# A one-core layer program whose separate preamble is spread over statistics, routing and experts

## What is computed

```python
x = x + 0.5 * ffn(layernorm(x), waff, W1, b1, W2, b2, threshold)
x = x + attn(layernorm(x), W_qkv, u_qkv, sigma_qkv, W_proj, u_proj, sigma_proj)
x = x + 0.5 * ffn(layernorm(x), waff, W1, b1, W2, b2, threshold)
```

```python
v = W @ u;    v = v / norm(v)
u2 = W.T @ v; u2 = u2 / norm(u2)
sigma = einsum('c,cd,d->', v, W, u2)
y = x @ (sigma_param[0] / sigma * W)
```

```python
num = einsum('bsd,ed->bse', inputs, waff)
aff = num / (norm(inputs) * norm(waff) + 1e-9)
cap = clip(floor(S * sigmoid(aff.mean() - threshold)), 4, S)
dispatch = one_hot(argmax(aff)) * (rank of aff in its sequence < cap)
for e in range(8):
    out += gelu((inputs * dispatch[e]) @ W1[e] + b1[e]) @ W2[e] + b2[e]
```

## Time and profile before

| what | us |
| --- | --- |
| median of 3 runs without profile | 1116.17 (1114.18 to 1118.52) |
| the profiled execution | 1130.24, of it the span 1128.4 |
| preamble, to the first load of x | 0.8 to 42.35 |
| statistics | 42.35 to 95.28 |
| routing | 95.28 to 165.87 |
| first experts, until PE's last dense stretch | 165.87 to about 330 |
| attention, settling of places, second experts | to the end |

### The profile page before, as it was taken

One profiled execution on the slowest core, in us unless ns is written; L12 is line 12 of the kernel. 1 busy time (PEld: TensorE's weight loads), 2 busy tenths in 40 slices (PEclk: granted clock), 3 DMA queues, 4 the chain that ended last, 5 costly groups with the idle time before them and its releaser, 6 DMA issues. The chain is left out here.

```text
span 1128.4 us, 26562 instructions
## 1 busy us (share of the span) xinstructions
PE 920.1 (82%) x8217; PEld 692.7 (61%) x8217; DVE 722.5 (64%) x2357; ACT 592.5 (53%) x1548; POOL 710.2 (63%) x1318
## 2 busy tenths in 40 slices
PE   2494636999965789999899998999999883799996
PEld 1383225999962456656556565565655552699995
DVE  6587953444423668887887878788888764344441
ACT  3023513666631456666666655666666561466663
POOL 4261975444303457888888877888888674155554
PEclk9755556999995989999999999999999995799998
DMA  5261002222314554554554545445455300222220
GB/s 168 84 189 32 1 5 45 68 68 68 64 41 94 99 90 91 95 115 93 100 113 92 101 88 103 95 97 115 94 104 108 70 22 23 69 65 67 59 66 22
DMA packets 127407, 89.72 MB, mean 80 GB/s; under 512 B 14305, under 2 KB 117910, under 8 KB 127270
## 3 DMA queue, kind: packets, MB, share of 16 engines
q1 hardware_dynamic: 104166, 53.24, 22.1%
q10 hardware_dynamic: 14400, 17.19, 7.9%
q0 software_dynamic: 8704, 17.60, 5.8%
HBM read 52.23 MB, written 35.47 MB: 78 GB/s over the span
## 5 line engine op out<-in xcount | busy, mean ns | idle before, releaser
L1529 DVE TENSOR_REDUCE at_mx<-at_pp 128x2 f32<-128x512 f32 (+1 forms) x384 | 261.8, 684 | 89.8 <-PE at_pp L1296 44.5
L1221 ACT ACTIVATE at_pt<-at_pm 128x512 f32<-128x512 f32 x384 | 228.7, 597 | 161.8 <-PE at_pm L1307 91.3
L1128 POOL TENSOR_SCALAR_AFFINE_SELECT at_pt<-at_pt 128x256 f32<-128x256 f32 (+1 forms) x384 | 184.8, 486 | 73.5 <-ACT at_pt L1221 69.9
L877 ACT ACTIVATE e_ht<-e_ps_h,b1t 128x128 f32<-128x128 f32 x576 | 164.2, 370 | 90.3 <-PE e_ps_h L905 78.1
L905 PE MATMUL e_ps_h<-e_xnt,e_w1own 128*128 128x128 f32 x1152 | 157.5, 281 | 7.0 <-issue 3.6
L915 PE MATMUL e_ps_y<-w,e_ht 128*128 x1152 | 160.3, 283 | 1.0 <-issue 1.0
L905 PEld LDWEIGHTS e_ps_h<-e_xnt,e_w1own 128*128 128x128 f32 x1152 | 144.9, 198 | 9.0 <-issue 7.3
L915 PEld LDWEIGHTS e_ps_y<-w,e_ht 128*128 128x128 f32 x1152 | 140.9, 193 | 2.2 <-issue 0.5
L961 DVE SCALAR_TENSOR_TENSOR e_y<-e_ps_y,e_x 128x256 f32<-128x256 f32 x72 | 30.6, 425 | 163.6 <-PE e_ps_y L915 163.6
L843 POOL DMA_INDIRECT out_dram<-e_y,e_x x72 | 73.9, 1026 | 94.7 <-DVE e_y L961 81.7
L827 POOL DMA_INDIRECT e_x<-rows,gidx x72 | 68.5, 951 | 75.0 <-DVE e_y L961 56.3
(11 more groups left out here) (331 smaller groups left out, 1802.1 us busy)
## 6 DMA issues: line engine op xcount, KB each, us to landing
at_qkd<-at_part SPq DMA_DIRECT2D x64, 192.0 KB
kb<-at_qkd SPq DMA_DIRECT2D x64, 96.0 KB
qs<-at_qkd ACTq DMA_DIRECT2D x64, 96.0 KB
e_x<-buckets SPq DMA_DIRECT2D x72, 66.0 KB
x<-e_y SPq DMA_DIRECT2D x36, 128.0 KB
rows<-ts_x ACTq DMA_DIRECT2D x16, 264.0 KB, 2.9
ts_x<-in_x_dram SPq DMA_DIRECT2D x16, 256.0 KB
x_by_token<-at_xa SPq DMA_DIRECT2D x32, 128.0 KB
```

The costliest lines, as they stand in the source:

```text
L877: last = a.activation(hid_t[j % NB][:, f, :], ps_h[j % NB][:, f, :], ACT.Gelu, bias=c.b1t[:, ds(e, 1), f])
L1128: g.affine_select(out=tile, in_=tile, compare_op=ALU.is_ge, fill=0.0, base=0, pattern=[[0, n], [1, P]], channel_multiplier=-1).then_inc(ma ...
L1221: a.activation(pt[u % RING][:, :], pm[u % 2], ACT.Exp, scale=SCALE).then_inc(exped, 1)
L1529: v.tensor_reduce(out, src, axis=AX.X, op=ALU.max).then_inc(maxed, 1)
```

## The change

The block `preamble` is gone. Its work stands elsewhere:

- In `token_stats` the ring has eight buffers. ACT's queue issues the ten small loads, the router weights and b1 first (semaphore `w_in`), the other eight counted by `s_in`. POOL makes the identity, the blank columns of the eight buffers and the iotas ahead of its roots, and the other constants after the root of one block or another (`constant`). DVE fills the small blanks before its first block, does `small` between the statistics of blocks 0 and 1, and a piece of the spectral norm after the normalization of most blocks (`spectral`). PE's small matmuls stand behind the projection of blocks 0, 4, 9 and 13. ACT takes gelu(b1) at the start and writes the constant rows of `kb` after blocks 4, 6, 8 and 10.
- In `route` SP loads w2 and w1 at the block's start. The 32 bias matmuls stand in groups of eight behind the inversions of groups 3 to 6, into PSUM that the counts no longer need; the sum over experts stands before the last inversion. DVE adds up behind its eight groups and makes the three parts after the expert numbers; SP then writes `cst`. Four small tiles now share memory with `den`, which is no longer needed there.
- In the first `experts` POOL blanks `kb`, `qs` and `vp`, 16 pieces, one behind the gathers of units 3 to 18 (`blank`). PE waits once for w2, DVE once for w1.
- The memsets of a ninth, empty expert in w1 and w2 are gone.

The diff, cut to this:

```diff
-        NX = 4
+        NX = 8
...
+            def power(n):
+                if n == 0:
+                    pool.wait_ge(early, 3)
+                    pool.wait_ge(powask, 1)
+                    g.tensor_tensor(c.wnorm[:, :], sq[:, :], half[:, :], ALU.pow).then_inc(pows, 1)
+                else:
+                    pool.wait_ge(powask, n + 1)
+                    g.tensor_tensor(col[:, 6 + 2 * n:8 + 2 * n], col[:, 4:6], mhalf[:, :], ALU.pow).then_inc(pows, 1)
+
+            def constant(b):
...
+                if b == 3:
+                    power(0)
+                if b == 7:
+                    power(1)
+                if b == 13:
+                    power(2)
...
                 g.tensor_tensor(c.xnorm[:, ds(b * TS, TS)], x_row[k][:, :, D + 1], x_row[k][:, :, D + 2], ALU.mult).then_inc(xnorm_done, 1)
+                constant(b)
...
+            a = nc.scalar
+            act.dma_start(waff_n[:, :], io["waff"]).then_inc(w_in, 16)
+            act.dma_start(b1_chunks[:, :], io["b1"].rearrange("e (c p) -> (e c) p", p=P)).then_inc(w_in, 16)
+            for dst, src in ((w_raw[:, parts[0]], io["wqkv"]), (w_raw[:, parts[1]], io["wproj"]),
+                             (u_row[:, parts[0]], io["uqkv"].partition_broadcast(P)), (u_row[:, parts[1]], io["uproj"].partition_broadcast(P)),
+                             (sig[:, 0:1], io["sqkv"].partition_broadcast(P)), (sig[:, 1:2], io["sproj"].partition_broadcast(P)),
+                             (c.thr[:, :], io["thr"].partition_broadcast(P)), (c.b2_rows[:, :], io["b2"])):
+                act.dma_start(dst, src).then_inc(s_in, 16)
+            act.wait_ge(filled, 4)
+            act.wait_ge(b1_t, 1)
...
+                if b in (4, 6, 8, 10):
+                    minus_one((b - 4) // 2)
...
+            def small():
...
+                dve.wait_ge(waff_tr, 1)
+                v.tensor_copy(c.waff_t[:, :], p_small[:, 0:E]).then_inc(waff_done, 1)
+                dve.wait_ge(waff_done, 1)
+                v.tensor_tensor(sq[:, :], c.waff_t[:, :], c.waff_t[:, :], ALU.mult).then_inc(ask, 1)
+
+            def spectral(b):
+
+                if b == 1:
+                    dve.wait_ge(picked, 2)
+                    v.tensor_reduce(sel_f[:, :], pick[:, :, :], axis=AX.X, op=ALU.add).then_inc(sel_done, 1)
+                    dve.wait_ge(told, 1)
+                    v.tensor_copy(sq[:, :], p_small[:, 16:16 + E]).then_inc(powask, 1)
+                    dve.wait_ge(s_in, 16 * 8)
+                    s.step(v.tensor_tensor(prod[:, :], w_raw[:, :], u_row[:, :], ALU.mult))
+                if b == 2:
+                    dve.wait_ge(sel_done, 1)
+                    for w in range(2):
+                        v.tensor_copy(sel[:, :, w], sel_f[:, :]).then_inc(selected, 1)
+                    s.step(sums(0))
+                if b == 3:
+                    v.tensor_tensor(col[:, 2:4], col[:, 0:2], col[:, 0:2], ALU.mult).then_inc(ask, 1)
+                if b == 5:
+                    dve.wait_ge(told, 2)
+                    v.tensor_copy(col[:, 4:6], p_col[:, 0:2]).then_inc(powask, 1)
+                if b == 8:
+                    dve.wait_ge(pows, 2)
+                    s.step(v.tensor_tensor(col[:, 0:2], col[:, 0:2], col[:, 8:10], ALU.mult))
+                    s.step(v.tensor_scalar(v_bc[0][:, :], c.ones[:, :], col[:, 0:1], None, ALU.mult))
+                    v.tensor_scalar(v_bc[1][:, :], c.ones[:, :], col[:, 1:2], None, ALU.mult).then_inc(ask, 1)
+                if b == 10:
+                    dve.wait_ge(told, 3)
+                    s.step(v.tensor_copy(u2[:, :], p_u2[:, :]))
+                    s.step(v.tensor_tensor(prod[:, :], u2[:, :], u2[:, :], ALU.mult))
+                if b == 11:
+                    sums(4).then_inc(powask, 1)
+                    dve.wait_ge(powask, 3)
+                    s.step(v.tensor_tensor(prod[:, :], w_raw[:, :], u2[:, :], ALU.mult))
+                if b == 12:
+                    s.step(sums(6))
+                    v.tensor_tensor(col[:, 2:4], col[:, 6:8], col[:, 0:2], ALU.mult).then_inc(ask, 1)
+                if b == 14:
+                    dve.wait_ge(told, 4)
+                    dve.wait_ge(pows, 3)
+                    s.step(v.tensor_tensor(col[:, 12:14], p_col[:, 0:2], col[:, 10:12], ALU.mult))
+                    s.step(v.reciprocal(col[:, 12:14], col[:, 12:14]))
+                    s.step(v.tensor_tensor(col[:, 14:16], col[:, 12:14], sig[:, :], ALU.mult))
+                if b == 15:
...
                 if not last:
                     stats(b + 1, (k + 1) % NX)
                 norm(b, k)
+                spectral(b)
...
+            def spectral(b):
+                if b == 0:
+                    pe.wait_ge(early, 1)
+                    pe.wait_ge(ask, 1)
+                    te.matmul(p_small[:, 16:16 + E], c.ones[:, :], sq[:, :], start=True, stop=True).then_inc(told, 1)
+                if b == 4:
+                    pe.wait_ge(ask, 2)
+                    te.matmul(p_col[:, 0:2], c.ones[:, :], col[:, 2:4], start=True, stop=True).then_inc(told, 1)
+                if b == 9:
+                    pe.wait_ge(ask, 3)
+                    for w in range(2):
+                        last = te.matmul(p_u2[:, parts[w]], v_bc[w][:, :], w_raw[:, parts[w]], start=True, stop=True)
+                    last.then_inc(told, 1)
+                if b == 13:
+                    pe.wait_ge(ask, 4)
+                    te.matmul(p_col[:, 0:2], c.ones[:, :], col[:, 2:4], start=True, stop=True).then_inc(told, 1)
...
                     project(b - 1, (k - 1) % NX)
+                spectral(b)
...
+            pe.wait_ge(eye, 2)
+            pe.wait_ge(w_in, 16 * 2)
+            te.transpose(p_small[:, 0:E], waff_n[:, :], c.ident[0:E, 0:E]).then_inc(waff_tr, 1)
+            te.transpose(p_b1[:, 0:E * FC], b1_chunks[:, :], c.ident[0:E * FC, 0:E * FC]).then_inc(b1_t, 1)
+            pe.wait_ge(waff_done, 1)
             run(step)
...
+        @blk.sync
+        def _(sp):
+            sp.dma_start(c.w2[:, 0:E, :, :], io["w2"].rearrange("e (c p) d -> p e c d", p=P)).then_inc(c.w2_in, 16)
+            sp.dma_start(c.w1[:, 0:E, :], io["w1"].rearrange("e d f -> d e f")).then_inc(c.w1_in, 16)
+            sp.wait_ge(const_split, 5)
+            for n in range(3):
+                sp.dma_start(c.cst[n:n + 1, :, :], c.const_parts[:, n, :].unsqueeze(1)).then_inc(c.cst_in, 16)
...
+            def bias_rows(q):
+
+                if q == 0:
+                    pe.wait_ge(c.w2_in, 16)
+                    pe.wait_ge(coords, 1)
+                for n in range(q * E, (q + 1) * E):
+                    last = te.matmul(own, c.gelu_b1[:, n * E:(n + 1) * E], c.w2[:, n // FC, n % FC, :],
+                                     start=(n == 0), stop=(n == E * FC - 1))
+                if q == FC - 1:
+                    last.then_inc(bias_sum, 1)
...
                 if g >= INV_LAG:
                     invert(g - INV_LAG)
+                if BIAS <= g < BIAS + FC:
+                    bias_rows(g - BIAS)
             for g in range(NG - INV_LAG, NG):
+                if g == NG - 1:
+                    pe.wait_ge(b2_done, 1)
+                    te.matmul(both, c.ones[0:E, 0:G], c.b2_rows[:, :], start=True, stop=True).then_inc(bias_done, 1)
...
             carry(NG - 1)
+            dve.wait_ge(zeroed, 1)
+            dve.wait_ge(bias_sum, 1)
+            v.tensor_copy(own_rows[0:E, :], own_of).then_inc(own_done, 1)
+            dve.wait_ge(own_done, 1)
+            v.tensor_tensor(c.b2_rows[:, :], c.b2_rows[:, :], own_rows[0:E, :], ALU.add).then_inc(b2_done, 1)
...
+
+            dve.wait_ge(bias_done, 1)
+            v.tensor_tensor(const_rows[:, :], both_of, own_rows[:, :], ALU.subtract).then_inc(const_done, 1)
+            dve.wait_ge(const_done, 1)
+            for n in range(3):
+                rows = const_rows if n == 0 else rest_rows
+                v.tensor_copy(c.const_parts[:, n, :], rows[:, :]).then_inc(const_split, 1)
+                if n < 2:
+                    dve.wait_ge(const_split, 2 * n + 1)
+                    v.tensor_tensor(rest_rows[:, :], rows[:, :], c.const_parts[:, n, :], ALU.subtract).then_inc(const_split, 1)
...
@@ -834,6 +859,8 @@
                     if j % 2 == 0:
                         pool.wait_ge(y_done, j // 2 + 1)
                     gather(j + 2 * NR)
+                    if j % 2 == 1 and 3 <= j // 2 < 3 + 4 * NQ:
+                        blank(j // 2 - 3)
...
             pe.wait_ge(c.cst_in, 16 * 3)
+            pe.wait_ge(c.w2_in, 16)
...
-        preamble(nc, m, io, c)
         token_stats(nc, m, io, c, io["x"])
-        route(nc, m, c, "r1")
+        route(nc, m, io, c, "r1")
```

352 lines of the change are left out of this document (126 added, 226 removed).

## The result

| | before | after |
| --- | --- | --- |
| median of the runs, us | 1117.35 (4 runs, 1114.18 to 1120.91) | 1081.67 (4 runs, 1080.78 to 1082.42) |
| the profiled execution | 1130.24 | 1081.78, of it the span 1080.0 |

The ratio is 0.9676, with a 95% interval of 0.964 to 0.9713: 35.7 us shorter, between 32 and 40. The forecast was 1084.4 in a range of 1076 to 1093, with 31.8 us less. So it holds, and most of its terms hold one by one; those of the ring and of routing don't, and their errors have opposite signs.

The account below looks back on a forecast made before the run. Bound by a serial preamble chain (41.55 us), then DVE in statistics, POOL in routing, PE in experts. Terms -41.55 + 0.5 + 8.2 - 3.6 + 1.6 + 2.4 + 0.3 = -32.15, scaled to 31.8: 1084.4 us, range 1076 to 1093.

Parts of the forecast that it names:

- The first rows later: Start of statistics: first rows land 3.4 us after issue instead of 2.87, sharing DMA engines; +0.5 us, bounds 0 and 2.
- The rival of small loads that hold up the first blocks: Start of statistics: small loads land late behind rows, DVE stands until 11.8; +6 us, 1090; chance 0.13.
- The moved DVE work: Statistics: preamble work moved between blocks of DVE, which sets the pace, counts in full; +8.2 us.
- The ring of eight: Statistics: eight row buffers instead of four take back all of DVE's waits for row loads; -3.6 us, bounds -3.6 and 0.
- DVE's wait for u2: Statistics, block 10: DVE stands for PE's large matmul (u2); +1.6 us, bounds 0 and 2.5.
- The tail of the stage: End of statistics: four scaled weights, about 1.3 us, hide in DVE's 5.34 us idle before routing; 0.
- Routing: Routing: bias matmuls at the slow rate and DVE's bias work add 9.9 us, 7.46 to spare; +2.4, bounds 0 and 5.
- The issues of the bias rows: End of routing: three issues of the bias rows, 2.42 us, end together with DVE's last index work; +0.3 us.
- Experts: Experts: POOL's 16 blank fills between gathers, some 16 us, cost nothing as PE sets the pace; 0, up to +2.
- rival (c): Statistics and experts: DVE and POOL block each other at a shared port; +3.5 us, 1088; chance 0.09.
- Rival (b): Statistics and routing: routing and the spectral wait (u2) are free, PE at quick rate; -4.0 us, 1080; chance 0.16.
- (d): Experts: PE's work at a granted clock of 0.50 makes the kernel slower than before, 1129; chance 0.02.

Follow-up runs that it names:

- e_dve2: Changed kernel with two products and two row sums of the spectral norms done twice on DVE; median 35.9 us below the kernel before.
- b_ring8: Kernel before with eight row buffers in statistics instead of four and nothing else of the change; median 7.6 us below the kernel before.
- e_ring4: Changed kernel with the ring of row buffers four deep again instead of eight; median 39.0 us below the kernel before.
- e_bias2: Changed kernel with the 32 bias matmuls of routing done twice; median 31.4 us below the kernel before.
- e_pool4: Changed kernel with four of POOL's 64 comparisons in routing done by DVE; median 41.3 us below the kernel before.
- e_blank2: Changed kernel with each of POOL's 16 blank pieces in the experts filled twice; median 34.3 us below the kernel before.

## Why the prediction was right

By its own steps, each with what the traces show:

- **The start, -41.55: right.** The first load is issued at 0.80.
- **The first rows later, +0.5: right.** 3.16 us from issue to statistics instead of 2.87, +0.3. The rival of small loads that hold up the first blocks (+6) did not come as described: the router weights never kept DVE waiting. The other small loads did, in block 1.
- **The moved DVE work, +8.2: right.** Statistics are 7.74 longer on DVE. Taken from it: 2.25 and 1.33 of new waits and 0.5 of two small ones, 0.4 of two `vare` additions that took 0.41 and 0.37 instead of 0.17 beside POOL's selects; put back: 3.6 of row waits and 1.2 of waits for roots that are gone. That leaves 8.0. e_dve2 shows that such work counts in full.
- **The ring of eight, -3.6: wrong in its place.** In the kernel before it gives 4.0 (b_ring8). In the changed kernel it gives nothing (e_ring4 begins routing 0.8 earlier). The step that failed is the sentence that all 3.6 come back: 3.6 went and 2.25 came, its net is -1.35, and the wait of the product in block 1 for the small loads stood nowhere in the sum. With four buffers that wait is gone (e_ring4), and DVE's longer blocks leave only 1.8 us of waits for rows instead of 3.6. The step's own comparison was loose too: 8.5 MB in 50 us are 170 GB/s, a little more than the 162 of before, not less; the stage ran at 148.
- **DVE's wait for u2, +1.6: right**, 1.33.
- **The tail of the stage, 0:** 6.06 instead of 5.34, +0.7 that I had not seen. Half of it is PE, which had no gap left behind its last small matmul: it begins the last transposes 1.52 us behind the start of the last normalization instead of 1.15. The other 0.3 lies between ACT's last copy and routing (1.34 instead of 1.01); what takes it is open.
- **Routing, +2.4: wrong.** It is -0.3. What failed is the level: the step took the slow rate for all four groups, as routing had it before, when PE had less to do. Only the first group ran at it, and there the step is nearly right: DVE stood 2.61 us where it says 2.15, the rest being 3.55 instead of 3.06 for 16 rows (its 3.06 was half of 32 rows in which the rate rose). The other three took 1.91, and the inversions before them 0.91 instead of 1.62, so that the slack was 2.1 there, not 1.3 (e_bias2). So DVE stood 2.6 us in place of 7.4; with its 2.5 us of bias work that stays inside the 7.46 it had to spare, and POOL's 45.5 us ended routing as before (e_pool4).
- **The issues of the bias rows, +0.3: wrong, 0**, since DVE ended later than they did; with a longer routing they do count (e_bias2).
- **Experts, 0: right**, though the lockout of rival (c) exists with memsets and costs 3.3 with twice as many (e_blank2). In statistics (c) was not put to the test: in after no power was running at any of the three products (13.40, 41.22, 45.30).

The start of routing came 32.8 us earlier and the first gather 33.1, against a sum of 32.15. What made the sum good is that its errors cancel, and that is luck. Too little or nothing was put down for the small loads (2.25), the tail (0.7) and the small waits and slower additions (0.9), 3.9 in all; too much for routing and its issues (3.0), the waits for roots that went (1.2), u2 (0.3), the moved work (0.2) and the first rows (0.2), 4.9 in all. The median moved by 35.7 against a forecast of 31.8; the 3 to 6 us beyond the stages are in no term, and where they come from is open. Rival (b), with routing free, was half true: PE was quick, the wait for u2 was not free. The fear of a slow clock (d) has nothing in the traces: from 160 to 291 us PE is full at a granted 1.00, as it was before; nor has that of a start that does not shorten (e).

## What to carry to other kernels

A serial preamble is worth nearly its whole length if the rest of the program has the time on other engines; here 41.55 us came off and 8 were paid back on the engine that sets the pace. Count what a shared semaphore makes an instruction wait for: one product paid 0.6 to 2.4 us for four loads that it didn't need. And a deeper ring that helps one order of loads can do nothing in another, because it puts more bytes ahead of the loads beside it.

## What the runs showed of the hardware

- A granted clock of 1.00 in the table does not mean quick rows. In after it stands at 1.00 from the start to 118 us, yet four transposes take 1.09 us in statistics, as they do at 0.50 in the kernel before, and the first group of 16 bias rows takes 3.55 (in e_dve2 3.45 at a printed 0.50); from 102 us on 16 such rows take 1.91. PE was busy without a gap from 96.2 to that point. Until the column first changes, rows tell which of the two levels (1.2 or 2.4 GHz) holds, not the column.
- One chip of three let PE stand for 4 to 5 us, with one to three single matmuls 1 to 3 us apart in it, 2 to 4 us after its rows had become quick in the experts; the granted clock then fell back to 0.50. It did so in all four kernels of its set, and the first profile of before shows the same. The cause is open.
- A POOL memset of 96 x 2048 elements (1.82 us) held a DVE copy for up to 2 us (2.47 instead of 0.42, e_blank2).
